# Decoder kernel: stacked query and key halves kept in device memory as planes of 128 rows, loaded one head at a time

## What is computed

```
k = 0 splat   q, k -> exp(-|q - c|^2 * s) features, 16 per head, 256 keys
k = 1 cross0  head size 16, 120 context keys
k = 2 causal  head size 16, 256 keys, causal
k = 3 self1   head size 32, 256 keys, softmax over all keys, mask applied after it
k = 4 cross1  head size 32, 120 context keys
attention:    softmax(scale * q k^T) v, out projection, residual, layer norm
between:      a gated expert layer before k = 2, GELU layers after k = 3 and k = 4, a top-4 expert layer at the end
```

## Time and profile before

| | |
|---|---|
| three executions | 3819.16 to 3821.56 us, median 3819.78 us |
| the profiled execution | 3815.62 us |
| its span, first to last instruction | 3813.5 us |
| granted TensorE clock, mean | 0.915 |
| PE matmul busy | 3122.0 us, 82% |
| DVE busy | 2700.8 us, 71% |
| ACT busy | 2106.9 us, 55% |
| GpSimd busy | 978.6 us, 26% |
| DMA | 221.30 MB, 58 GB/s over the span |
| setup before the first matmul | 62.4 us |

### The profile page before, as it was taken

How to read it: one execution, slowest core, us unless ns; L and a number is a source line. 1 busy time by engine, 2 the same in 40 slices (tenths; PEclk the granted TensorE clock), 3 DMA queues, 4 the chain that set the end, 5 groups by cost and what they waited for, 6 DMA issues and landing times. The chain is left out here.

```text
span 3813.5 us, 88266 instructions
## 1 busy us (share of the span) xinstructions
PE 3122.0 (82%) x34864; PEld 2454.4 (64%) x34864; DVE 2700.8 (71%) x6135; ACT 2106.9 (55%) x4254; POOL 978.6 (26%) x1793
## 2 busy tenths in 40 slices
PE   2988788888788878878988878798978898978886
PEld 1767566767576766656766656676756676756664
DVE  5777676778675767757767658687767677858765
ACT  4745565555456555554565545546655556456652
POOL 1312341122222321231133222212333122124310
PEclk9999898989898989989999989899989998989987
DMA  6221211112112121121122111212211112112110
GB/s 196 70 57 51 73 56 60 46 46 67 53 52 66 44 66 44 48 64 54 47 62 64 54 51 38 68 46 68 61 57 60 44 41 69 48 57 68 60 38 6
DMA packets 337676, 221.30 MB, mean 58 GB/s; under 512 B 77409, under 2 KB 309234, under 8 KB 337266
## 3 DMA queue, kind: packets, MB, share of 16 engines
q1 hardware_dynamic: 337266, 215.66, 18.9%
HBM read 122.23 MB, written 93.32 MB: 57 GB/s over the span
## 5 line engine op out<-in xcount | busy, mean ns | idle before, releaser
L1159 ACT ACTIVATE p<-bank,p_log 128x512 f32<-128x512 f32 (+2 forms) x1280 | 749.3, 585 | 1188.8 <-PE bank L851 1087.9
L1713 POOL TENSOR_TENSOR prob<-p,prob 120x256 f16<-120x256 f32 (+2 forms) x512 | 451.0, 881 | 1709.5 <-ACT prob L1160 1709.1
L1418 DVE TENSOR_REDUCE negm<-bank 128x2 f16<-128x512 f32 (+1 forms) x1280 | 675.4, 569 | 167.5 <-PE bank L814 155.1
L1160 ACT ACTIVATE prob<-bank,p_log 128x512 f16<-128x512 f32 (+2 forms) x1280 | 750.5, 586 | 0.0
L721 PE MATMUL bank<-w_exp,ident_h 128*128 128x512 f16 x1280 | 421.3, 413 | 159.2 <-DMA k_ring<-k_heads 143.6
L1348 DVE TENSOR_TENSOR prob<-p,prob 128x512 f16<-128x512 f32 (+2 forms) x768 | 487.4, 644 | 90.3 <-ACT prob L1160 85.7
L830 PE MATMUL bank<-q_ring,k_ring 80*128 80x256 f16 (+4 forms) x2048 | 446.1, 285 | 39.0 <-ACT raw L1106 14.1
L851 PE MATMUL bank<-ident_h,negm 128*128 128x256 f16 (+2 forms) x2560 | 442.1, 260 | 0.0
L1722 POOL TENSOR_SCALAR_AFFINE_SELECT probm<-prob 128x128 f16<-128x128 f16 x1024 | 327.9, 359 | 315.0 <-DVE prob L1348 315.0
L814 PE MATMUL bank<-k_ring,q_ring 80*128 80x256 f16 (+4 forms) x2560 | 370.5, 260 | 35.4 <-DVE negm L1418 34.7
L814 PEld LDWEIGHTS bank<-k_ring,q_ring 80*128 80x128 f16 (+1 forms) x2560 | 237.5, 104 | 238.3 <-issue 55.4
(11 more groups left out here) (299 smaller groups left out, 6190.3 us busy)
## 6 DMA issues: line engine op xcount, KB each, us to landing
q_ring<-q_heads SPq DMA_DIRECT2D x384, 80.0 KB, 1.9
q_heads<-q_made SPq DMA_DIRECT2D x96, 256.0 KB
k_heads<-k_made SPq DMA_DIRECT2D x96, 256.0 KB
q_ring<-q_heads SPq DMA_DIRECT2D x256, 96.0 KB, 2.0
k_ring<-k_heads SPq DMA_DIRECT2D x256, 80.0 KB, 2.1
q_heads<-q_made SPq DMA_DIRECT2D x144, 128.0 KB
k_heads<-k_made SPq DMA_DIRECT2D x144, 128.0 KB
k_ring<-k_heads SPq DMA_DIRECT2D x128, 96.0 KB, 2.2
```

What stands on the lines that cost most here:

```text
L1159: act(p32[0:n, g % PBUF32, 0:cols], ps[0:n, 0:cols], ACT.Exp, bias=p_log[0:n, :], scale=a.scale)
L1160: act(prob[0:n, 0, g % PBUF, 0:cols], ps[0:n, 0:cols], ACT.Exp, bias=p_log[0:n, :], scale=a.scale).then_inc(a_done, one(a_done))
L1418: v.tensor_reduce(negm[:, h * NT:(h + 1) * NT], ring_v[bank_of(e, v_full)][:, :].rearrange("p (t n) -> p t n", t=NT)[:, :, 0:ATTNS[k].keys ...
L1713: g.tensor_tensor(prob[0:n, 1, m % PBUF, 0:cols], p32[0:n, m % PBUF32, 0:cols], prob[0:n, 0, m % PBUF, 0:cols], ALU.subtract).then_inc(pp_ ...
```

## The change

The two tensors in device memory become planes of 128 rows: (buffer, plane, partition of `made`, tile and token). A store writes one whole plane, whose outermost dimension is now the 128 rows. The five or three stacked rows that belong to one feature of one head are now `l` planes apart, and a fill reads one head with the feature outermost and the plane inside it, so the stacked rows in the ring are ordered feature by feature, the same way for q and k. A fill issues four DMAs (q and k of each of the two heads) in place of two, and `slot_filled` counts accordingly. The zeros are written as whole planes 3 and 4, 8 DMAs as before.

```diff
 def slot_filled(m):
-    return 2 * 16 * (m // SLOTS + 1)
+    return 2 * PAIR * 16 * (m // SLOTS + 1)
...
-        heads16 = {what: nc.dram_tensor(f"{what}_heads16", (2, 8, 80, 2, TOK), F16).ap() for what in "qk"}
-        heads32 = {what: nc.dram_tensor(f"{what}_heads32", (2, 4, 96, 4, TOK), F16).ap() for what in "qk"}
+        heads16 = {what: nc.dram_tensor(f"{what}_heads16", (2, 5, P, 2 * TOK), F16).ap() for what in "qk"}
+        heads32 = {what: nc.dram_tensor(f"{what}_heads32", (2, 3, P, 4 * TOK), F16).ap() for what in "qk"}
...
-                        for g0 in (0, 4):
-                            e.dma_start(heads16[what][buffer, g0:g0 + 4, 48:80].rearrange("g r t n -> r g (t n)"),
-                                        hidT[0:32, :, :, :].rearrange("r a t n -> r (a t n)").rearrange("r (g c) -> r g c", g=4)
-                                        ).then_inc(zeros_stored, 16)
+                        for plane in (3, 4):
+                            e.dma_start(heads16[what][buffer, plane].rearrange("(p a) n -> p (a n)", a=4),
+                                        hidT[0:32, :, :, :].rearrange("p a t n -> p (a t n)")).then_inc(zeros_stored, 16)
...
                     for plane, part in enumerate(PLANES[what]):
-                        e.dma_start(to[:, plane * a.dim:(plane + 1) * a.dim].rearrange("c d t n -> c d (t n)"),
-                                    made[what][:, part, 0:a.tiles, :].rearrange("p t n -> p (t n)")).then_inc(stored, 16)
+                        e.dma_start(to[plane], made[what][:, part, 0:a.tiles, :].rearrange("p t n -> p (t n)")
+                                    ).then_inc(stored, 16)
...
-                    t, c = h // a.together, h % a.together
-                    for what, ring, cols in (("q", q_ring, TOK), ("k", k_ring, a.keys)):
-                        e.dma_start(ring[0:a.stacked, m % SLOTS, :, 0:cols],
-                                    heads_dram(what, k, b)[c:c + PAIR, :, t, 0:cols].rearrange("c r n -> r c n")
-                                    ).then_inc(ring_full[m % SLOTS], 16)
+                    for at in range(PAIR):
+                        t, c = (h + at) // a.together, (h + at) % a.together
+                        for what, ring, cols in (("q", q_ring, TOK), ("k", k_ring, a.keys)):
+                            e.dma_start(ring[0:a.stacked, m % SLOTS, at, 0:cols],
+                                        heads_dram(what, k, b)[:, c * a.dim:(c + 1) * a.dim, t * TOK:t * TOK + cols]
+                                        .rearrange("l d n -> d l n")).then_inc(ring_full[m % SLOTS], 16)
```

## The result

The changed kernel takes 3753.29 us (median of four, 3749.78 to 3758.32), the kernel before 3819.5 us beside it: a ratio of 0.983, 95% interval 0.981 to 0.984, 66 us or 1.7% faster. Its profiled span is 3751.0 us against 3813.5, 62.5 us less. The forecast was 3757 us, within 3722 to 3798.

What follows compares the result with a forecast made beforehand. PE, busiest at 82%, was taken to wait for ring loads (143.6 us) queued behind slow stores. Savings 58.9 + 19.5 less losses 0.7, 2.9, 7 and 5 gave 62.8 us, so 3757 us, range 3722 to 3798.

Steps and rivals of the forecast that it cites:

- Cause of the slow stores: Stores to device memory: heads outermost use 4 or 8 of 16 DMA engines; 128 rows outermost should give all, 339 GB/s.
- A: Six PE waits at the first pair of self1, lane 0, head size 32, together 82.3 us: 58.9 us saved.
- B: Eight PE waits for loads landing behind a store of head size 32, together 19.5 us: all saved.
- C: Six PE waits at the first pair of cross0, lane 0, head size 16, together 30.1 us: nothing gained.
- D: PE's wait at the very first pair, 8.04 us: 0.7 us lost.
- I take 0.98, since issues of 80 to 256 KB all took 0.4 to 0.5.: SP's loads: four DMAs for two complete a pair 0.98 us later, if a half-sized DMA costs as much as a whole.
- E: Three small PE waits, placed at head size 16, together 3.6 us: 2.9 us lost.
- just-in-time loads: Quick stretches with pairs 1.5 us apart, less than four issues need: some ten pairs at 0.7 us, 7 us lost.
- clock term: After the long stalls, PE stays at the low clock level longer when stalls are shorter: 0.9 us each, 5 us lost.
- SP becomes the bound: Rival, chance 0.05: in quick pairs of cross0 and cross1, four issues exceed the pairs' distance; 3875 us, half of it 3816.
- Loads get slower: Rival, chance 0.11: a feature's rows lie farther apart in device memory, 1.7 us more at some 26 late pairs; 3801 us.
- More is saved: Rival, chance 0.08: half-sized issues cost half, small pairs lose nothing, C gains too; 3730 us.

Runs made afterwards that it cites:

- padded planes: The changed kernel with unused rows behind each head in every plane, so stores have 8 or 4 heads outermost again: 3873.72 us, ratio 1.014 to the kernel before.
- first experiment: Against the kernel before: head's rows feature by feature with planes inside, stores 128 rows outermost, pairs still loaded by two DMAs, zeros by 4: 3703.9 us, ratio 0.969.

## Why the prediction was right

The mechanism of the stores held, and the time of 3757 against 3753 is close. It is closer than its terms, and that is luck. My sum takes 67.8 us off PE's waits; they lost 57.8 (143.6 to 85.8). And it has a loss of 5 us outside the waits, for the clock, where there was a gain of 4.7 (62.5 us of the span less the 57.8). Two errors of 10 us cancel.

- **Cause of the slow stores.** Right: the share went from 0.25 to 0.92, the padded planes bring 0.26 back, and contiguous planes are not needed (first experiment). The Trainium skill's rule (DMA: Bandwidth & Descriptors, "Why a DMA increments its semaphore by 16 and not by 1") names the same quantity, the outermost dimension of both sides; by that rule, the trace agrees (0.25 and 0.26 with 4 heads outermost, 0.92 with 128 rows). One reading beside it was wrong: the engines in use did not move 25 GB/s each in both cases of the earlier trace rows, but 25 at a share of 0.25 and 21 at 0.56.
- **A**: 58.9 us forecast, 82.3 - 23.7 = 58.6 measured. Inside it two errors cancel: stores were ready in 3.4 us, not 4.0, and the pair came 1.4 us later, not 0.98. (The shortest of A before was 13.04, not 13.24.) **B**: 19.5 forecast, and all of it gone. **C** 0 forecast, 1.4 us gained, again as a small difference of two larger terms than I had: four of the six store paths 1.7 to 2.0 us shorter, not 1.0, and the pairs 1.6 to 2.5 us later, not 0.98. **D** 0.7 us lost forecast, 0.3 lost.
- **The step that was mis-sized: "I take 0.98, since issues of 80 to 256 KB all took 0.4 to 0.5."** The price of an issue was taken from rows with simple sources; the new load has three dimensions and costs SP 0.60 us. Four of them are 2.55 us of SP, not 1.96. Together with it the term for E and for just-in-time loads was too small: 2.9 + 7 = 9.9 us forecast, while the 26 small waits of the kernel after sum to 25.1 us against 3.6 before, 21.5 us: E's three are 1.68, 2.37 and 3.24, together 3.7 more, and 23 just-in-time pairs, not ten, wait 17.8. The price for one, 0.7 us, was right (0.77); the count was not. Nor was the place: the quick pairs of the earlier trace rows (2426.67 and 2428.18) and the third wait of E belong to a cross1 phase of head size 32, not to head size 16, and the new waits stand mostly outside cross0. The whole price of the loads, by the table, is 49 to 53 us, where my sum had 0.98 on 13 waits of A, C and D (12.7) and these 9.9, 22.6 us.
- **The stores' gain was sized too low as well**: 10.8 x 6 + 19.5 + 6 + 0.3 = 90.6 us in my terms, 117 to 120 by the table. In the first experiment, where beside the stores only the order of the rows and the writing of the zeros change, 103 us of it are waits of PE for loads. The span lost 113.
- **The clock term did not come out.** I counted 5 us lost because shorter stalls would leave PE longer at the low level. At the first wait of A they do. Stretches behind it, kernel after, where the earlier trace rows has 3.6 us at 0.51:

```profile
399.00:401.00 2.00, 1.87 (x27) 1.50 (x24) 1.27 (x3) 1.41 (x4) 0.00 (x0) 0.50 0.19 49
401.00:405.00 4.00, 3.81 (x16) 2.64 (x17) 1.52 (x3) 1.55 (x5) 0.91 (x1) 0.50 0.26 75
```

But over the span PE's busy time, which grows at that level, is 3123.4 us against 3122.0, while the mean granted clock rose from 0.915 to 0.924. The mean misleads: in the long stalls part of the low level fell into the stall itself (clock 0.67 with PE busy 0.00), where it costs nothing. In the first experiment PE's busy time is 3105.3 us at a mean clock of 0.929, 17 us less, more than the 10 us of the span that the waits leave unexplained. The kernels that lost go the other way: the waits of the padded one are 41 us more than before, its span 63 us longer, and PE's busy time 3149.6 us. So late loads seem to cost more than their waits, by way of the clock; one trace of each kernel says so, and no run tests it by itself.
- **"k_ring waits near 60 us"** did not even follow from my own sum, which takes 58.9 + 19.5 - 0.7 - 2.9 - 7 = 67.8 from 143.6 and so gives 76. Measured: 85.8.
- **The rivals.** "SP becomes the bound" is real in small: the waits near 3130 us have SP issuing without a pause. It cost less than the stores gained, but the padded kernel shows the same loads ending on the slow side when that gain is missing. "Loads get slower" through wider strides hardly showed: they land 2.2 us after issue, where loads of a pair took 1.9 to 2.2 and plain loads of one head 1.8 to 1.9; the rival had 1.7 us more. "More is saved" was right about the stores and wrong about the loads.

## What to carry to other kernels

Look at the DMA share beside the GB/s in a stretch where only one kind of transfer runs: in this kernel 0.25 was a transfer on 4 engines and 0.56 one on 8, and the remedy was a layout in which the 128 rows have one stride and are outermost, which need not be contiguous. Then keep the other side's transfers whole: here the two aims, fast stores and two loads per pair, fit in one layout (rows of a head ordered feature by feature, planes inside), and it beats both kernels (3704 us against 3753 and 3820). A queue that "waits most of the time" can still be late in the quick stretches, so count the issues per step against the shortest step, at the price that their own shape has.

## What the hardware showed that I had not expected

- The time that SP takes to issue one DMA, one behind another, depends on its shape: 0.43 us for 128 rows or for one head from a plain source, 0.45 for a pair of heads, 0.60 for a source of feature, plane and token, with the same or fewer bytes. Among the stores and loads of q and k, in all the rows at 0.43 to 0.45 the outermost dimension is the same on both sides (128 rows, or 80 or 96); in all those at 0.57 or more it differs (8 or 4 heads against 128, 16 or 32 features against 80 or 96, 5 or 3 planes against 80 or 96). This is a pattern and not a cause: no run tests it by itself, and the zeros of the kernel before, with 32 rows outermost on both sides and 4 heads inside, took 2.43 us for four and do not fit it. The number of dimensions alone does not order the rows either, since the load of a pair has three.
- It is longer in the rows where fewer engines are used: 0.57 to 0.60 us for a store over 4 or 8 engines (1.80 for three) against 0.43 over all (1.29 for three), and 0.68 against 0.60 for loads. That alone does not order the rows: the changed kernel's loads, with 16 or 32 features outermost, cost as much as stores over 4 or 8 engines. The Trainium skill, same page and section, says that for engines which a transfer doesn't use the issuing sequencer writes the semaphore's remaining counts itself. That would be such a cost; the rows show the longer issue, not its cause.
- A load's landing was little changed by its size or its stride: in the median 1.8 to 1.9 us (one head, plain), 1.9 to 2.2 (a pair), 2.2 (one head, three dimensions). What made it long was a store ahead of it: the 9.29 us of the earlier trace rows, in a wait of B, and all waits of B are gone with fast stores.
